# The projection of q and k transposed, their stacks rebuilt through DRAM, and a shorter latent path in half of the tiles

## What is computed

```
h = layernorm(x) * (1 + ca) + sa
q, k, v = split(h @ qkv_w + qkv_b)             # 16 heads of 16
local   = softmax(q k^T / 4, over the 128 tokens before) @ v
pooled  = mean of h over chunks of 16 tokens   # 64 latents a batch
lattn   = softmax(rq rk^T / 4, over the latents of earlier chunks)
remote  = (lattn @ rv) @ rout_w + rout_b
gate    = sigmoid(local @ gl_w + remote_h @ gr_w)
x       = x + ga * ((gate * local + (1 - gate) * remote_h) @ out_w + out_b)
h       = layernorm(x) * (1 + cb) + sb
x       = x + gb * ffn(h)
```

## Time and profile before

| | us |
|---|---|
| median of 3 runs | 657.01 (656.66 to 661.27) |
| the profiled execution | 658.29 |
| its span, first to last instruction | 656.5 |

### The profile page before, as it was taken

One profiled execution on the slowest core, in us unless ns is written; L12 is line 12 of the kernel. 1 busy time (PEld: TensorE's weight loads), 2 busy tenths in 40 slices (PEclk: granted clock), 3 DMA queues, 4 the chain that ended last, 5 costly groups with the idle time before them and its releaser, 6 DMA issues. The chain is left out here.

```text
span 656.5 us, 22130 instructions
## 1 busy us (share of the span) xinstructions
PE 566.5 (86%) x7535; PEld 415.4 (63%) x7535; DVE 503.8 (77%) x1390; ACT 484.9 (74%) x1066; POOL 417.7 (64%) x616
## 2 busy tenths in 40 slices
PE   2739999999979999999979999999979999999972
PEld 2237666776657666667756666766756666666651
DVE  5637888888868787888868788888868888888864
ACT  1687787778868787777768788777767778877760
POOL 3335566667756577766657576776656576677673
PEclk9879999999999999999989999999989999999986
DMA  8183000000000000000000000000000000000000
GB/s 262 63 292 96 2 2 2 11 10 10 11 15 9 10 10 7 6 10 10 10 15 10 9 10 11 10 2 10 10 15 10 9 10 11 10 6 6 11 18 16
DMA packets 13761, 17.48 MB, mean 27 GB/s; under 512 B 2980, under 2 KB 11836, under 8 KB 13628
## 3 DMA queue, kind: packets, MB, share of 16 engines
q1 hardware_dynamic: 10764, 14.52, 6.4%
q10 hardware_dynamic: 2864, 1.31, 0.8%
HBM read 11.61 MB, written 4.22 MB: 24 GB/s over the span
## 5 line engine op out<-in xcount | busy, mean ns | idle before, releaser
L554 ACT ACTIVATE pr<-p_y 128x512 f32<-128x512 f32 x232 | 135.0, 597 | 30.4 <-PE p_y L802 26.6
L1171 DVE TENSOR_REDUCE mtok<-p_x 128x3 bf16<-128x480 f32 (+3 forms) x192 | 113.5, 591 | 53.3 <-issue 29.6
L399 POOL TENSOR_SCALAR_AFFINE_SELECT pr<-pr 128x512 f32<-128x512 f32 x132 | 88.5, 670 | 49.7 <-ACT pr L554 46.0
L801 PE MATMUL p_y<-qst,kst 112*128 112x128 bf16 x464 | 71.3, 220 | 27.5 <-ACT pr L554 26.7
L403 POOL TENSOR_SCALAR_AFFINE_SELECT pr<-pr 128x512 f32<-128x512 f32 x116 | 89.7, 773 | 0.0
L802 PE MATMUL p_y<-qst,kst 112*128 112x128 bf16 x528 | 77.9, 219 | 3.1 <-ACT pr L556 3.1
L409 POOL TENSOR_TENSOR rstd<-ve,half 128x1 f32<-128x1 f32 x104 | 63.7, 620 | 26.5 <-DVE ve L1094 24.7
L427 POOL TENSOR_TENSOR dif<-local,rem 128x272 f32<-128x272 f32 x34 | 25.9, 762 | 85.0 <-DVE local L1224 85.0
L705 PE MATMUL p_qkv<-wqk,hT 128*128 128x512 f32 x136 | 69.1, 632 | 2.1 <-issue 1.2
L801 PEld LDWEIGHTS p_y<-qst,kst 112*128 112x128 bf16 x464 | 45.2, 101 | 40.4 <-issue 30.5
L545 ACT ACTIVATE qst<-p_x 96x1024 bf16<-96x1024 bf16 x66 | 67.3, 1019 | 2.5 <-PE p_x L748 0.5
(11 more groups left out here) (159 smaller groups left out, 1498.6 us busy)
## 6 DMA issues: line engine op xcount, KB each, us to landing
out_y<-y SPq DMA_DIRECT2D x32, 128.0 KB, 2.4
x_all<-in_x SPq DMA_DIRECT2D x1, 3072.0 KB, 17.9
pr<-in_wmod SPq DMA_DIRECT2D x1, 1024.0 KB, 10.1
row<-in_rows SPq DMA_DIRECT2D x1, 816.0 KB, 7.0
x_all<-in_x SPq DMA_DIRECT2D x1, 768.0 KB, 4.9
wqk<-in_qkv_w ACTq DMA_DIRECT2D x1, 512.0 KB, 3.8
pr<-in_wmod SPq DMA_DIRECT2D x1, 512.0 KB, 5.3
pr<-mod_rows SPq DMA_DIRECT2D x1, 512.0 KB, 4.0
```

The costliest lines, as they stand in the source:

```text
L399: ins = pool.affine_select(out=own, in_=own, compare_op=ALU.is_ge, fill=0.0, base=-1, pattern=[[0, 4], [1, P]], channel_multiplier=-1)
L554: act.activation(pr[:, 2 * i:2 * i + 2, :, :], src, ACT.Exp).then_inc(exp_done[i], 1)
L801: pe.matmul(p_y[i % 2][:, at:at + P], kst[0:KS + H, h, (n - 1) % NB, :], q, start=True, stop=True)
L1171: dve.tensor_reduce(mtok[:, KS + h0:KS + h1], p_x[i % 2][:, 0:(h1 - h0) * w].rearrange("p (h n) -> p h n", n=w), AX_X, ALU.max, negate=Tru ...
```

## The change

The projection is turned: for pairs of tiles, weights stationary and 256 tokens moving, so that q (in one slot) and k (in the next) come out as features by tokens. The three terms are formed in that form, one instruction a step (`terms`), for q and k in turn. SP stores the terms of a pair to DRAM (`store_terms`) and loads them back, head by head on 16 partitions a term, six loads for q and six for k (`load_stack`). The transposes and the stack copies are gone. Minus the maximum is one row that goes from `mrow` to `qst` by DMA (`shift`, now on SP), and `kst` has one row of ones, loaded once. The norm of a tile runs four slots ahead instead of two, and the start runs the slots -4 to -1. POOL has `res1` and `part3` ahead of the first mask, `add_bias` behind it, and `rstd3_of` ahead of the third. ACT has `part1` first and `part2` between the first two exponentials. The edge mask is four products of 32 columns. In the first four tiles of a batch the latent path works on 32 latents, the only ones that can be allowed there.

```diff
-Q_SLOTS = {1: (2, 5, 1), 2: (1, 6, 4), 3: (0, 1, 1)}
-K_SLOTS = {1: (0, 3, 1), 2: (3, 6, 2), 3: (4, 5, 1)}
-
+Q_TERMS = (0, 0, 0, 1, 1, 2)
+K_TERMS = (0, 1, 2, 0, 1, 0)
+LEAD = 4
...
+        qkf = sb("qkf", [P, 2, KC, 2 * P])
+        terms = sb("terms", [P, 2, 3, KC, 2 * P], BF16)
+        qst = sb("qst", [P, 2, H, 2 * P], BF16)
...
+        def seen(t):
+
+            return LT // 2 if t[1] % NB < NB // 2 else LT
...
             sp.dma_start(x_all[:, (XPAD + NB) * D:(XPAD + NT) * D].rearrange("p (t d) -> p t d", d=D),
                          x[NB:NT].rearrange("t p d -> p t d")).then_inc(loaded_x, 16)
 
+            def shift(t):
+                wait_apart(sp, (mrow_ready, done(t)), (st_psum[NP - 1], done(back(t, 4))))
+                sp.dma_start(q_of(t)[KS:KS + 1, :, :], mrow[:, :]).then_inc(shift_loaded[t[1] % 2], 16)
+
+            def store_terms(r):
+
+                half = r[1] % 2
+                wait_apart(sp, (part3_ready, done(r)), (stack_loaded[half], halves(back(r, 2), 16 * NTERM)))
+                sp.dma_start(scr[half].rearrange("t p n -> p t n"), terms[:, half, :, :, :].rearrange("p s b n -> p (s b) n"))\
+                  .then_inc(terms_stored[half], 16)
...
+            def load_stack(r):
+
+                half = r[1] % 2
+                pair = pair_of(r)
+                wait_apart(sp, (terms_stored[half], halves(r, 16)), (st_psum[NP - 1], done(back(r, 7 if half else 3))))
+                n = pair[1] % NB
+                for i in range(NTERM):
+                    if half:
+                        dst = kst[i * HD:(i + 1) * HD, :, n:n + 2, :].rearrange("d h r n -> d h (r n)")
+                    else:
+                        dst = qst[i * HD:(i + 1) * HD, n // 2 % 2, :, :]
+                    s0 = (K_TERMS if half else Q_TERMS)[i] * KC
+                    sp.dma_start(dst, scr[half][s0:s0 + KC].rearrange("b (h d) n -> d (b h) n", d=HD))\
+                      .then_inc(stack_loaded[half], 16)
...
+            def slot(t, stages):
+                r, m, d = back(t, -2), back(t, 1), back(t, 3)
+                Q, T, D_ = ("Q" in stages, "T" in stages, "D" in stages)
+                if T:
+                    shift(m)
+                if Q:
+                    store_terms(r)
+                if Q and t[1] % 2:
+                    load_stack(r)
+                if D_:
+                    store(d)
+                if Q and t[1] % 2 == 0:
+                    load_stack(r)
+
+            slot((0, -2), "Q")
+            slot((0, -1), "Q")
+            for n in range(NB):
+                slot((0, n), "QT" if n < 3 else "QTD")
...
             def res1(t):
 
                 pool.wait_ge(part1_ready, done(t))
-                pool.tensor_tensor(heads(res[:, 0:D]), heads(qkf[:, 0:D]), slots(qtok, Q_SLOTS[1])[:, :, 0, :], ALU.subtract)
-                pool.tensor_tensor(heads(res[:, D:2 * D]), heads(qkf[:, D:2 * D]), slots(ktok, K_SLOTS[1])[:, :, 0, :],
-                                   ALU.subtract).then_inc(res_ready, 1)
+                half = t[1] % 2
+                pool.tensor_tensor(qkf[:, half, :, :], qkf[:, half, :, :], terms[:, half, 0, :, :], ALU.subtract)\
+                    .then_inc(res_ready, 1)
 
             def part3(t):
+
                 pool.wait_ge(part2_ready, done(t))
-                pool.tensor_tensor(slots(qtok, Q_SLOTS[3])[:, :, 0, :], heads(res[:, 0:D]),
-                                   slots(qtok, Q_SLOTS[2])[:, :, 0, :], ALU.subtract)
-                pool.tensor_tensor(slots(ktok, K_SLOTS[3])[:, :, 0, :], heads(res[:, D:2 * D]),
-                                   slots(ktok, K_SLOTS[2])[:, :, 0, :], ALU.subtract).then_inc(part3_ready, 1)
+                half = t[1] % 2
+                pool.tensor_tensor(terms[:, half, 2, :, :], qkf[:, half, :, :], terms[:, half, 1, :, :], ALU.subtract)\
+                    .then_inc(part3_ready, 1)
...
                     add_u(d)
+                if A:
+                    rstd1(a)
+                if Q:
+                    res1(r)
+                if D:
+                    rstd2_of(d)
+                if Q:
+                    part3(r)
+                if T:
+                    mask(m, 0)
                 if C:
                     add_bias(c)
-                if A:
-                    rstd1(a)
-                if D:
-                    rstd2_of(d)
-                if T:
-                    mask(m, 0)
-                if K:
-                    part3(k)
-                if C:
                     difference(c)
                 if T:
                     mask(m, 1)
-                    mask(m, 2)
                 if D:
                     rstd3_of(d)
                 if T:
+                    mask(m, 2)
                     mask(m, 3)
-                if A:
-                    res1(a)
...
             def part1(t):
 
+                half = t[1] % 2
                 act.wait_ge(qk_copied, done(t))
-                act.wait_ge(stack_psum[3], done(back(t, 1)))
-                act.activation(slots(qtok, Q_SLOTS[1]), rep(qkf[:, 0:D], Q_SLOTS[1]), ACT.Copy)
-                act.activation(slots(ktok, K_SLOTS[1]), rep(qkf[:, D:2 * D], K_SLOTS[1]), ACT.Copy).then_inc(part1_ready, 1)
+                act.wait_ge(terms_stored[half], halves(back(t, 2), 16))
+                act.activation(terms[:, half, 0, :, :], qkf[:, half, :, :], ACT.Copy).then_inc(part1_ready, 1)
...
             def part2(t):
+
+                half = t[1] % 2
                 act.wait_ge(res_ready, done(t))
-                act.activation(slots(qtok, Q_SLOTS[2]), rep(res[:, 0:D], Q_SLOTS[2]), ACT.Copy)
-                act.activation(slots(ktok, K_SLOTS[2]), rep(res[:, D:2 * D], K_SLOTS[2]), ACT.Copy).then_inc(part2_ready, 1)
+                act.activation(terms[:, half, 1, :, :], qkf[:, half, :, :], ACT.Copy).then_inc(part2_ready, 1)
...
+                if Q:
+                    part1(r)
                 if C:
                     out_t(c)
                 if T:
                     lat_oT(m)
-                if K:
-                    part2(k)
-                if T:
                     exps(m, 0)
+                if Q:
+                    part2(r)
+                if T:
                     exps(m, 1)
                 if S:
...
                     exps(m, 6)
-                if K:
-                    stack_copy(k, 0)
-                    stack_copy(k, 1)
-                if T:
                     exps(m, 7)
+                if S:
+                    lat_pT(t)
                 if C:
                     mixed_t(c)
-                if K:
-                    stack_copy(k, 2)
-                if A:
-                    part1(a)
-                if S:
-                    lat_pT(t)
-                if K:
-                    stack_copy(k, 3)
...
+            def project_half(t):
+
+                pair, half = pair_of(t), t[1] % 2
+                pe.wait_ge(hT_ready, done(back(pair, -1)))
+
+                pe.wait_ge(rem_ready, done(back(t, 4)))
+                pe.wait_ge(v_copied, done(back(t, 2)))
+                pe.wait_ge(qk_copied, done(back(t, 1)))
+                r = pair[1] % 4
+                for b in range(KC):
+                    for k in range(KC):
+                        ins = pe.matmul(p_qkv[:, 2 * b * P:2 * (b + 1) * P], wqk[:, k, half * D + b * P:half * D + (b + 1) * P],
+                                        hT[:, r:r + 2, k, :], start=(k == 0), stop=(k == KC - 1))
                 ins.then_inc(qk_psum, 1)
...
             def scores(t, i):
 
-                if i == 0:
-                    pe.wait_ge(stack_copied[0], done(t))
-                    pe.wait_ge(stack_copied[1], done(t))
-                    pe.wait_ge(stack_copied[2], done(t))
-                elif i == 1:
-                    pe.wait_ge(stack_copied[3], done(t))
-                else:
-                    pe.wait_ge(s_max[i - 2], done(t))
+                if i == 0 and t[1] % 2 == 0:
+                    for half in range(2):
+                        pe.wait_ge(stack_loaded[half], halves(back(t, -half), 16 * NTERM))
+                pe.wait_ge(s_max[(i - 2) % NS], done(t if i >= 2 else back(t, 1)))
                 n = t[1] % NB
...
-                    pe.matmul(ends, ident_bf[:, :], edge[:, :].unsqueeze(1).to_broadcast([P, h1 - h0, 2 * QG]).rearrange("p h (e n) -> p h e n", n=QG),
-                              start=True, stop=True)
+                    for g in range(4):
+                        pe.matmul(ends[g * QG:(g + 1) * QG], ident_bf[:, g * QG:(g + 1) * QG],
+                                  edge[:, :].unsqueeze(1).to_broadcast([P, h1 - h0, 2 * QG]).rearrange("p h (e n) -> p h e n", n=QG),
+                                  start=True, stop=True, tile_position=(0, g * QG))
...
             def scores_t(t, i):
 
-                pe.wait_ge(shift_ready, done(t))
+                pe.wait_ge(shift_loaded[t[1] % 2], halves(t, 16))
                 pe.wait_ge(exp_done[(i - 2) % NP], done(t if i >= 2 else back(t, 1)))
...
```

(62 more changed lines are left out.)

291 lines of the change are left out of this document (125 added, 166 removed).

## The result

The changed kernel takes 802.84 us (median; 800.65 to 812.47) against 657.55 (656.66 to 661.27) in runs on the same chip: ratio 1.222, 95% interval 1.213 to 1.232. It is slower. The forecast was 734, its range 680 to 815. The profiled execution took 800.8 us for a span of 798.8. Of the two runs of the later kernel with loads over more partitions, the profiled one was in a slower state of the chip, so its time in the table is the other run's.

The account below looks back on a forecast made before the run. It took a slot to be held by PE's stream and a nearly equally long loop of short steps through four engines. Profiled 658.3 + 0 (loop order) + 40 (late shift) + 37 (start) = 735, less 1.3: 734 us; range 680 to 815.

Parts of the forecast that it names:

- The start: Before the main loop: first scores wait for both stacks behind modulation rows and x, at 84 instead of 47.3, +37 us.
- The order of short steps: Main loop through four engines: what PE and ACT save becomes waiting; quiet slot 17.8 to 18.0 against 17.86, costed at nothing.
- The load: Stack loads on SP: 768 KB in six DMAs, 7.0 us from first issue to last landing; q's runs into the next slot.
- The rival of the sixteen partitions: Stack loads: sixteen partitions cut the rate, 10 to 12 us each; loop +88 to +120, total 785 to 830; chance 0.18.
- The step that failed: Odd slots: the maxima row, queued behind the q load, lands at +5.6 instead of +3.1, 2.5 us late; +40 us over 32 slots.
- the summed path: Whole kernel: the late shift as summed, 734 us, its own range 705 to 760; chance 0.43.
- The k load: Odd slots: follows `part3` and the store, lands at about +16.5, before the next slot needs it.
- The end: After the main loop: the same three drain slots, costed at nothing.
- PE alone decides: Main loop: short steps fall below PE's stream, slots 14.5 to 15.5, loop gains 75 to 105, total 575 to 620; chance 0.12.

Follow-up runs that it names:

- The three kernels on the start: Changed kernel with x issued early, 794.4 us; with rows and x behind the stacks, 796.5; with x early, 96-partition loads and q load behind the shift, 673.4.
- with the transfers out of the way: Changed kernel with 96-partition loads, q load behind the odd slot's shift, and x and first q load early at the start: 673.4 us, ratio 1.020.
- the three fastest forms of the changed kernel: Changed kernel with 96-partition loads, q load behind shift, new start: 673.4 us; plus ACT's sixth exponential ahead of tanh: 650.0; plus DVE's `local_out` early: 636.1.
- the latent part alone: Kernel before with 32 latents in the first four tiles, pooled rows written once and maximum negated in one instruction; stacks still by transposes: 650.0 us, ratio 0.986.

## Why the prediction was right, and where it was wrong

**The start: right, term by term.** Modulation rows at 42.77 (I had 32.44 + 11), x at 48.10 (48.9), q loads at 66.67 (68.5 for the store's landing), first scores at 83.65 (84), +36.35 against +37. The three kernels on the start show the order on SP to be the cause of two thirds of it: 74.7, 59.3 and 58.9. The 11.6 us that are left beside 47.30 go to k's stack, which the last of them stores only at 47.40, and to its load, for which the scores wait.

**The order of short steps: right in the sum, wrong in where the slot is held.** I costed it at nothing; with the transfers out of the way it is +1.4 in 31 slots, the latent part's 8.3 included, of which I had 0.2 in half of the slots. But the quiet slot is 16.85 to 17.89 and not 17.8 to 18.0, and POOL's refinement ahead of the mask comes earlier than I had it: in the slot from 421.68, `scores_t` begins at +2.8 (I had +3.1), the mask is done at +6.8 (+7.5), `add_eps3` comes at +12.8 (+13.7). Each link came a little earlier than costed, above all the row of maxima. The other chain that I read in the earlier trace rows and left as it was, `local`, `dif`, tanh, sixth exponential, gave 23 and 14 us when it was reordered, most of the 23 at the turn of the batches. That the whole is even hides that boundary slots lost what quiet ones gained (20.5 against 17.4 to 19.0 behind the loop's turn).

**The load: in its place, but too short.** I took 7.0 us from first issue to last landing, a first issue 1.7 us ahead of the odd slot, and a landing at +5.3. The issue is 1.5 ahead in the mean of the 14 slots. The bulk is through in 6.6 to 7.0 us, but the last landing comes after 8.2 to 9.1, 8.6 in the mean, at +7.0. Pieces left over on the DMA engine that a fetch of instructions holds take 1.0 to 1.7 us of that in twelve of the slots, and I had no term for them. The rival of the sixteen partitions put it at 10 to 12, and the total fell into that rival's 785 to 830, in part by that road: 113 GB/s on sixteen partitions, and a bulk of 4.8 us instead of 6.8, worth 54 us in all, when one load writes 96. The Trainium skill, "SBUF — State Buffer", section "Door 1: The DMA port swizzle", gives 104 GB/s for partitions 0 to 15; the trace's 113 agrees with it to a tenth.

**The step that failed: the length of the load, and what a late row costs.** That the row lands 0.3 us after the load was right in the mean: 0.15 to 0.17 in twelve of the 14 odd slots, 1.3 in the two where the fetch comes between them. But with the load at +7.0, `scores_t` starts at +6.4 to +8.6, 7.4 in the mean, and not at +5.6; without collision it is 2.8. That is 4.6 late instead of 2.5. A row that meets no load lands 1.7 us after its issue (I had 2.3). The Trainium skill, "DMA: Bandwidth & Descriptors", section "Anatomy of one DMA — SWDGE (gpsimd) path", puts a fixed cost of about 2.0 us on each DMA, most of it the wait for the write's receipt; the 1.7 us here are near it, on SP's queue, though that page measured another path. Then I let 2.5 us late cost 2.5 us. The 14 slots are late by 14 x 4.6 = 65 us and longer by 95; the other 30 stand beside granted clocks of 0.62 to 0.92 in these slots. In the slot from 438.00, PE is busy for 20.24 us with work that takes 14.49 in the next slot. That the clock fell because PE had stood still is argued from rows: PE idle 440.7 to 446.3, 0.50 from there on; no run varied the clock alone. So +40 should have been about +100. That 802.84 lies in the range at all is luck: the summed path had a range of its own to 760, and the range reached 815 only to take in the sixteen partitions.

**The k load:** hidden in the odd slot, as said; the run with both loads in one slot shows how little room it had. **The end** cost 2.8 us and not nothing; 31.0 to 31.2 us remain in the three fastest forms of the changed kernel, 30.0 with the latent part alone, and its cause stays open. **PE alone decides** did not happen, and could not by that edit: the chain through POOL and ACT was left as it stood.

## What to carry to other kernels

A small DMA that an engine waits for in every pass must not be queued, or in flight, with a large one: put the large one behind it. Time the large one to its last landing, not to the end of its bulk: both land only when the last of the 16 DMA engines has done its part. Price a wait of the matrix engine by what it does at the lower clock afterwards as well; here 4.6 us of it cost 6.8. And before work is taken off the busiest engine, follow its one marked wait back to the engine where a ready instruction stands behind a waiting one: here two reorderings moved the time by 37 us, and the 32 transposes a slot by none that the sum shows.

## What the runs showed of the hardware that I had not expected

- A fetch of 16 KB of instructions holds one of the 16 DMA engines for 0.9 to 2.0 us. In the kernel after, a load spread over all of them then lands 8.2 to 9.1 us after its issue though its bulk is through in 6.6 to 7.0, and the 4 KB behind it with it.
- A DMA issued on another engine's queue does not pass the bulk of a load that keeps the DMA engines busy: 6.0 us to landing instead of 1.7 for 4 KB.
- Six loads that together cover 96 partitions run at the rate of sixteen, 113 GB/s, since they follow each other; one load over 96 partitions moves the bulk of the same 768 KB in 4.8 us.
- SP itself can stand still in one issue: 10.84 us for the 384 KB store behind 3 MB of rows and 3 MB of x, 11.13 for a row of 4 KB behind 2.5 MB of rows and x.
- After 5.6 us without work, PE was granted 0.50 for the 18.8 us that were left of the slot, though it was busy for 17.6 of them.
